# Turning the second batch's normalised rows through HBM and VectorE in an attention and mixture-of-experts kernel

## What is computed

```python
xn = layernorm(x)
qkv = xn @ w_qkv.T + b_qkv; q, k, v = split(qkv)
s = softmax(q @ k.T / sqrt(512)) @ v @ w_out.T + b_out
logits = xn @ router_w + router_b           # 8 experts, top 2, softmax of the two
combined = sum over the 2 experts of weight * silu(xn @ expert_w[e] + expert_b[e])
y = xn + combined @ proj_w + proj_b
g = silu(norm_w * y / sqrt(mean(y * y) + 1e-6))
out = x + s * g
```

## Time and profile before

| | before |
|---|---|
| median of 3 runs | 485.66 us (485.57 to 486.53) |
| profiled execution | 484.21 us |
| its span, first to last instruction | 482.5 us |
| TensorE (PE) busy | 474.7 us, 98% |
| VectorE (DVE) busy | 315.7 us, 65% |
| ScalarE (ACT) busy | 214.0 us, 44% |
| GpSimd (POOL) busy | 217.6 us, 45% |
| TensorE's mean granted clock | 0.997 of full |
| DMA | 115.79 MB, 240 GB/s mean |

### The profile page before, as it was taken

How to read it: one execution, slowest core, us unless ns; L and a number is a source line. 1 busy time by engine, 2 the same in 40 slices (tenths; PEclk the granted TensorE clock), 3 DMA queues, 4 the chain that set the end, 5 groups by cost and what they waited for, 6 DMA issues and landing times.

```text
span 482.5 us, 7168 instructions
## 1 busy us (share of the span) xinstructions
PE 474.7 (98%) x2168; PEld 391.9 (81%) x2169; DVE 315.7 (65%) x471; ACT 214.0 (44%) x310; POOL 217.6 (45%) x318
## 2 busy tenths in 40 slices
PE   9999999999999999999999999999999999999995
PEld 7878777888888888888888888888888888888884
DVE  4965352776734446898888889753588665857653
ACT  3673563143230264644644444333655452554540
POOL 5685010007887859500400000664478873476234
PEclk9999999999999999999999999999999999999998
DMA  8956999956979599978789666996555874455412
GB/s 312 353 210 253 382 348 410 357 186 235 324 243 334 186 320 308 285 212 259 230 269 263 201 191 176 338 315 246 151 176 174 239 198 151 123 190 172 149 46 86
DMA packets 78192, 115.79 MB, mean 240 GB/s; under 512 B 6657, under 2 KB 36369, under 8 KB 78161
## 3 DMA queue, kind: packets, MB, share of 16 engines
q1 hardware_dynamic: 65072, 79.72, 52.5%
q0 software_dynamic: 6896, 23.36, 13.9%
q10 hardware_dynamic: 6192, 12.32, 7.3%
HBM read 66.09 MB, written 49.28 MB: 239 GB/s over the span
## 4 chain that ended last, share of the span: by engine, by line
PE 97%; DVE 1%; issue 1%; ACT 0%; DVEq 0%
PE ab L1662 22%; PE ab L1664 22%; PE ab L1663 22%; PE sc L1662 8%; PE sc L1664 7%; PE sc L1663 7%; PE tp L1668 2%; PE tp L1704 1%; PE tp L1763 1%; PE sc L1733 1%; PE sc L1774 1%; PE sc L1736 1%; PE ab L1686 0%; PE ab L1688 0%; DVE xt_l L1229 0%
## 5 line engine op out<-in xcount | busy, mean ns | idle before, releaser
L822 POOL DMA_INDIRECT y<-y_scratch,pos x32 | 33.3, 1042 | 77.7 <-DMA y_scratch<-yt_so 63.3
L1664 PE MATMUL ab<-W,st_l 128*128 x156 | 60.7, 389 | 0.0
L1663 PE MATMUL ab<-W,st_h 128*128 x156 | 60.7, 389 | 0.0
L1662 PE MATMUL ab<-W,st_h 128*128 x156 | 60.7, 389 | 0.0
L805 POOL DMA_INDIRECT rows_scratch<-xb,pos x32 | 31.2, 975 | 51.2 <-DVEq L1343 43.0
L1662 PE MATMUL sc<-xt_h,t_h 128*128 128x512 f32 x128 | 50.1, 391 | 0.0
L1664 PE MATMUL sc<-xt_h,t_l 128*128 128x512 f32 x128 | 49.9, 390 | 0.0
L1663 PE MATMUL sc<-xt_l,t_h 128*128 128x512 f32 x128 | 49.8, 389 | 0.0
L1081 ACT CAST st_h<-tp 128x512 fp32r<-128x512 f32 x39 | 22.9, 587 | 43.3 <-PE ab L1664 41.2
L1423 DVE TENSOR_REDUCE small<-sc 128x1 f32<-128x1024 f32 x16 | 19.5, 1221 | 24.7 <-PE sc L1664 24.4
L1664 PEld LDWEIGHTS ab<-W,st_l 128*128 128x128 f32 x156 | 29.3, 188 | 6.1
(11 more groups left out here) (286 smaller groups left out, 1227.4 us busy)
## 6 DMA issues: line engine op xcount, KB each, us to landing
rows_scratch<-xn ACTq DMA_DIRECT2D x3, 3328.0 KB, 20.1
xb<-in_expert_w POOLq DMA_DIRECT2D x6, 1024.0 KB, 10.1
xn<-rows_scratch SPq DMA_DIRECT2D x48, 128.0 KB, 3.1
xg<-rows_scratch SPq DMA_DIRECT2D x44, 128.0 KB, 3.1
y_scratch<-yt_own SPq DMA_DIRECT2D x20, 256.0 KB, 3.1
y_scratch<-yt_so SPq DMA_DIRECT2D x19, 256.0 KB, 3.1
p_scratch<-prob SPq DMA_DIRECT2D x9, 512.0 KB, 2.8
rows_scratch<-xs SPq DMA_DIRECT2D x16, 256.0 KB, 6.7
```

What stands on the lines that cost most here:

```text
L822: pool.indirect_dma_start(y[:, q, :], None, y_d, bass.IndirectOffsetOnAxis(pos[:, GB * s + p:GB * s + p + 1], 0))\
L1662: nc.tensor.matmul(dst, lh, rh, start=start, stop=False)
L1663: nc.tensor.matmul(dst, lh, rl, start=False, stop=False)
L1664: return nc.tensor.matmul(dst, ll, rh, start=False, stop=stop)
```

## The change

For batch 1 alone (tiles 8 to 15):

- ScalarE normalises each tile in place in `xb1`, so that its `normalise` waits for no slot of the ring `xs`. `row_stats` of batch 1 run one iteration earlier in the batch 0 loop.
- TensorE no longer transposes them. SyncE stores each tile as before, waits until a pair has landed, loads the pair back spread with four DMAs into `xb` (batch 0's x, dead by then), and VectorE transposes it into `tp` (`turn_spread`).
- The second half of batch 1 is split into `wk_h` and `wk_l` (free after the folds) and not into `bt_h` and `bt_l` again.
- TensorE's order of logits becomes (0,0), (0,1), (1,0), two `key_weights`, (1,1).
- ScalarE issues the first store of zeros alone; SyncE issues the other two, after the last spread load.
- The scatters begin with batch 1, straight from `xb1`; only batch 0's rows are reloaded.
- GpSimd's first two expert weight loads (into `xb`) wait for all turned tiles and not for the last normalised one.

```diff
@@ sync @@
+            def spread_pair(n):
+                g = GB + 2 * n
+                for k in (g, g + 1):
+                    sp.wait_ge(xn_st[k % 4], 16 * (k // 4 + 1))
+                for a in range(4):
+                    sp.dma_start(xb[32 * a:32 * (a + 1), 2 * n:2 * n + 2, :].rearrange("p t (r f) -> p (t r) f", r=4),
+                                 rows_q[home(g):home(g) + 2, a, :, :, :].rearrange("t s r f -> s (t r) f"))\
+                        .then_inc(x_in[n], 16)
...
-            for g in range(G):
+            for g in range(GB):
...
+            for g in range(GB, GB + 4):
+                store_row(g)
+            for n in range(KC):
+                spread_pair(n)
+                if n < 2:
+                    store_row(GB + 4 + 2 * n)
+                    store_row(GB + 5 + 2 * n)
+            for n in (1, 2):
+                clear_slots(sp, n)
...
-            for g in range(GB):
-                load_to_send(g)
@@ gpsimd @@
-            pool.wait_ge(xn_ready, G)
+            pool.wait_ge(t_done, G)
...
-            for g in range(G):
-                pool.wait_ge(send_in[g % GB], 16 * (g // GB + 1))
+            for n in range(G):
+                g = (n + GB) % G
+                if n >= GB:
+                    pool.wait_ge(send_in[g], 16)
@@ scalar @@
-                if g >= 4:
+                if 4 <= g < GB:
...
+                if g >= GB + QB:
+                    act.wait_ge(fold, 2 * KC)
...
-                if t >= GB - 3:
+                if t == GB - 3:
                     act.wait_ge(zero_set, 1)
-                    clear_slots(t - GB + 3)
+                    clear_slots(act, 0)
             act.wait_ge(ln_done, 3)
-            for g in range(GB, GB + 4):
+            for g in range(GB, GB + 6):
                 normalise(g)
             fold_high(KC)
             act.wait_ge(vecs, 2)
             nc.scalar.copy(bias_rows, ...)
+            normalise(GB + 6)
+            act.wait_ge(qk_split, 4)
             hi(GB)
+            normalise(GB + 7)
             hi(GB + 1)
             fold_high(KC + 1)
-            normalise(GB + 4)
-            normalise(GB + 5)
             hi(GB + 2)
             hi(GB + 3)
             fold_high(KC + 2)
-            normalise(GB + 6)
-            normalise(GB + 7)
             fold_high(KC + 3)
-            act.wait_ge(rt_done, 1)
             for g in range(GB + QB, G):
                 hi(g)
@@ vector @@
+            def turn_spread(g):
+                k = g - GB
+                dve.wait_ge(x_in[k // 2], 64 + 16 * (2 if k < 4 else 1))
+                dve.wait_ge(lo_done, g - 1)
+                vec.transpose(tp[:, g % 2, :, :].rearrange("p c (r s) -> p c r s", r=4),
+                              xb[:, k, :].rearrange("p (r q c) -> p c r q", r=4, c=KC)).then_inc(t_done, 1)
...
+            turn_spread(GB)
+            turn_spread(GB + 1)
             fold_low(KC)
             lo(GB)
+            turn_spread(GB + 2)
             lo(GB + 1)
+            turn_spread(GB + 3)
+            fold_biases()
             fold_low(KC + 1)
-            fold_biases()
             lo(GB + 2)
+            turn_spread(GB + 4)
             lo(GB + 3)
+            turn_spread(GB + 5)
             fold_low(KC + 2)
             fold_low(KC + 3)
-            for g in range(GB + QB, G):
-                lo(g)
+            lo(GB + 4)
+            turn_spread(GB + 6)
+            lo(GB + 5)
+            turn_spread(GB + 7)
+            lo(GB + 6)
+            lo(GB + 7)
@@ tensor @@
             bias_products()
-            turn(GB)
-            turn(GB + 1)
             fold_keys(FOLDS[1])
             turn_biases()
-            turn(GB + 2)
-            turn(GB + 3)
             fold_keys(FOLDS[2])
             fold_keys(FOLDS[3])
             pe.wait_ge(pre_done, 4)
-            pe.wait_ge(lo_done, GB + QB)
-            pe.wait_ge(fold_l, KC + 1 + FOLDS.index(2))
-            logit_rows(1, 0).then_inc(rt_done, 1)
-            turn(GB + QB)
-            turn(GB + QB + 1)
             pe.wait_ge(fold_l, KC + 1 + FOLDS.index(0))
             logit_rows(0, 0)
-            turn(GB + QB + 2)
-            turn(GB + QB + 3)
             pe.wait_ge(fold_l, KC + 1 + FOLDS.index(1))
             logit_rows(0, 1).then_inc(rt_done, 1)
+            pe.wait_ge(lo_done, GB + QB)
+            logit_rows(1, 0)
             pe.wait_ge(fold_l, 2 * KC)
             key_weights(0, 0, 0)
+            key_weights(0, 0, 1)
             pe.wait_ge(lo_done, G)
             logit_rows(1, 1).then_inc(rt_done, 1)
-            key_weights(0, 0, 1)
             key_weights(0, 0, 2)
```

More of the change, by code:

```diff
@@ L394, in by_fours, with turned_rows, clear_slots @@
             return v.rearrange("p (c q) -> p q c", c=KC)
+        def turned_rows(g):
+            w = slice(g % QB * P, (g % QB + 1) * P)
+            if g < GB:
+                return xt_h[:, :, g * P:(g + 1) * P], xt_l[:, :, g * P:(g + 1) * P]
+            if g < GB + QB:
+                return bt_h[:, :, w], bt_l[:, :, w]
+            return wk_h[:, :, w], wk_l[:, :, w]
+        def clear_slots(eng, n):
+            w = slice(n * SLOT_TILES // 3, (n + 1) * SLOT_TILES // 3)
+            eng.dma_start(rows_t[:, w, :], zeros.to_broadcast([P, w.stop - w.start, D])).then_inc(zero_in, 16)
         def weights(e):
@@ L532, in store_row @@
                 sp.wait_ge(xn_ready, g + 1)
-                sp.dma_start(rows_g[home(g)], xs[:, g % 4, :]).then_inc(xn_st[g % 4], 16)
+                sp.dma_start(rows_g[home(g)], xs[:, g % 4, :] if g < GB else xb1[:, g - GB, :])\
+                    .then_inc(xn_st[g % 4], 16)
+            def spread_pair(n):
[6 more added lines that the diff above has]
+                        .then_inc(x_in[n], 16)
             load_half(0)
-            for g in range(G):
+            for g in range(GB):
                 if g == 4:
@@ L544, in load_to_send @@
             def load_to_send(g):
-                if g >= GB:
-                    sp.wait_ge(sent[g % GB], 32)
-                sp.dma_start(sent_rows[:, g % GB, :], rows_g[home(g)]).then_inc(send_in[g % GB], 16)
+                sp.wait_ge(sent[g], 32)
+                sp.dma_start(sent_rows[:, g, :], rows_g[home(g)]).then_inc(send_in[g], 16)
             def load_pair(i, n, tiles=2):
@@ L590, in _ @@
             store_s(0)
-            for g in range(GB, GB + 4):
+            for g in range(4):
                 load_to_send(g)
             store_s(1)
-            load_to_send(GB + 4)
-            load_to_send(GB + 5)
+            load_to_send(4)
+            load_to_send(5)
             store_s(2)
-            load_to_send(GB + 6)
-            load_to_send(GB + 7)
+            load_to_send(6)
+            load_to_send(7)
             store_s(3)
@@ L806, in _ @@
                                             sent_rows[:, g % GB, :], None).then_inc(sent[g % GB], 16)
[L807 to L810, removed]
+                if n < 2 * KC:
+                    early_low(n // KC, n % KC)
+                elif n >= 3 * KC:
+                    early_low(2, n % KC)
             for c in range(KC):
@@ L911, in normalise @@
             def normalise(g):
[L912 removed]
+                if 4 <= g < GB:
                     act.wait_ge(t_done, g - 3)
                     act.wait_ge(xn_st[g % 4], 16 * (g // 4))
[L915 removed]
+                whole = xbs[g // GB][:, g % GB, :]
+                nc.scalar.activation(xs[:, g % 4, :] if g < GB else whole, whole, ACT.Identity, bias=shift[:, g:g + 1],
                                      scale=rstd[:, g:g + 1]).then_inc(xn_ready, 1)
@@ L935, in t_hi @@
                     .then_inc(ab_hi, 1)
-            def clear_slots(n):
-                w = slice(n * SLOT_TILES // 3, (n + 1) * SLOT_TILES // 3)
-                act.dma_start(rows_t[:, w, :], zeros.to_broadcast([P, w.stop - w.start, D])).then_inc(zero_in, 16)
             for c in range(1, KC):
@@ L1387, in _ @@
                     fold_value_bias()
-                if 2 <= t < 6:
-                    n = t - 2
+                if 1 <= t < 5:
+                    n = t - 1
                     for k in range(2 * n, 2 * n + 2):
@@ L1727, in logit_rows @@
             def logit_rows(b, m):
-                high, low = (xt_h, xt_l) if b == 0 else (bt_h, bt_l)
+                high, low = (xt_h, xt_l) if b == 0 else (bt_h, bt_l) if m == 0 else (wk_h, wk_l)
                 keys = slice(m * 512, (m + 1) * 512) if b == 0 else slice(0, 512)
```

10 lines of the change are left out of this document (4 added, 6 removed).

## The result

| | before | changed |
|---|---|---|
| median | 485.95 us (485.23 to 486.53, 6 runs) | 489.21 us (488.11 to 489.71, 6 runs) |
| profiled execution | 484.21 us, span 482.5 | 489.3 us, span 487.6 |
| TensorE's mean granted clock | 0.997 | 0.987 |

The changed kernel takes 1.0061 times as long (95% interval 1.0048 to 1.0075): slower by 3.3 us. The spans differ by 5.1 us, because the profiled execution of before lies 1.7 us under its median and that of the changed kernel on its own.

The account below looks back on a forecast made before the run. TensorE, busy 474.7 of 482.5 us, was taken as the bound. Saved work -4.2, new waits +5.2 and restarts +0.3 gave +1.3 us; on 485.66 that made 487.0 us, range 484.6 to 490.0.

Parts of the forecast that it names:

- TensorE never waits, so what is taken off it counts in full: TensorE, whole run: longest wait 1.1 us, at the start; removed transposes 3.9 us, in all 4.2 us saved.
- The first spread pair at x = 56.4: VectorE's first transpose of a reloaded batch 1 pair begins at 56.4 us, bounds 54.9 to 60.6; tile stores landed at 51.9.
- Rival 1: Zeros don't hold the tile stores: VectorE begins at 54.9, TensorE waits 3.7, sum -0.2 us, 485.5 us; chance 0.25.
- VectorE's chain of 13.1 us: VectorE's work from its first spread transpose to the end of fold 1's low part: 13.1 us.
- TensorE asks at 62.4 and 64.3: TensorE could begin logits (0,0) at 62.4 us and logits (0,1) at 64.3 us if operands were there.
- the formula: TensorE's waits before logits (0,0) and (0,1) together: x + 13.1 - 64.3, which is x - 51.2 = 5.2 us.
- Rival 4, the clock: Clock falls in TensorE's new waits: 1.9 us more for one set of logits, 3.7 for two; 488.9 to 490.7; chance 0.12.
- the two waits have work between them: Argument against a clock fall in TensorE's new waits of 2.5 and 2.7 us before the logits.
- Rival 3, the moved zeros: Moved zeros in SyncE's queue make the store of probabilities 0 land 2.7 late; 488.2 to 489.2 us; chance 0.10.
- my 97 for the end of the backlog: The 13.1 MB of zeros, `nw`, `mw` and expert weights, at 387 GB/s, gone 34 us later, at 97 us.
- the 1.5 us that I said would hide it: Slack for probabilities 0: `pt_l` of tile 0 done at 107.0, TensorE begins `attend_tile(0)` at 108.53.
- The carried-over 1.45 us: The runs' median stands 1.45 us above the profiled execution before the change; this difference was added to the forecast.

Follow-up runs that it names:

- kept-busy kernel: The changed kernel plus 22 unread matmuls on TensorE, 14 before logits (0,0) and 8 before logits (0,1); 490.32 us, 1.0081.
- reordered kernel: The changed kernel with the fold stretch's work in another order on VectorE, ScalarE and TensorE, in several forms; 489.96, 489.56, 482.81 and 482.90 us.
- kept busy with zeros early: The changed kernel with 22 unread TensorE matmuls and the first two stores of zeros on ScalarE in iterations 2 and 5; 488.02 us, 1.0035.
- rows stored before: The changed kernel with spread loads reading batch 0's rows, stored long before, so they needn't wait for batch 1's stores; 485.27 us, 0.9984.
- the first reordered one: The changed kernel, same DMAs and instructions, VectorE doing folds' low parts early with transposes between, logits turned last; 489.96 us, 1.0086.
- the kernel with all zeros late: The changed kernel with the first store of zeros on SyncE too, all three behind the spread loads; 495.15 us, 1.0193.

## Why the prediction was right, by its own steps

It forecast slower, 487.0 us in a range of 484.6 to 490.0; 489.21 came. The place was right, the size lies in the range's upper part, and that it lies inside at all is in part luck, as the last item says.

- **TensorE never waits, so what is taken off it counts in full.** Right: the 3.9 us stand in the balance as they were read from the earlier trace rows.
- **The first spread pair at x = 56.4.** It was 58.45. ScalarE's normalisations ended on time (the first two stores were issued from 47.89, forecast 48.3 for the second). The mis-sized term is the stores: landed by 54.15, forecast 51.9. They took 5.5 us, between the 2.0 and the 7.7 of the earlier trace rows. Rival 1, with its 54.9, is refuted: without any zeros x was 56.0, with its stretch 0.6 earlier, and a tile's store took 3.7 us for 5.5. So the zeros hold the stores by 1.8 us, but a store in a burst of tiles isn't 2.0 us even with the DMA quiet; it is 3.7. The 4.6 us from landing to transpose of the earlier trace rows were 4.3.
- **VectorE's chain of 13.1 us.** 12.8 from 58.45 to the end of fold 1's low part at 71.3. Right. That ScalarE's high parts stand behind the same transposes was not in the prediction; they cost nothing here.
- **TensorE asks at 62.4 and 64.3.** At 62.9 and 64.8, later by 0.5, of which 0.4 is the stretch's later beginning. In the formula, 64.8 for 64.3 and 71.36 for 69.5: 6.6 us in place of 5.2. Two waits were forecast, 2.5 and 2.7; there were 3.9 and 0.8. With the later x the first became longer, and the second shorter, since the slow clock stretched the work between them.
- **Rival 4, the clock.** I gave it 0.12, and it is what came. Its price for one set of logits, 1.9 us, is what was measured (1.9 in the balance, 2.0 by the kept-busy kernel). The step that failed is "the two waits have work between them": the first alone was long enough, since the clock fell within it, and in three experiments so was a single wait of 2.3 to 2.4 us. The tail of the earlier trace rows had shown a fall about 2 us after the work ceased; I had the row and gave it too little.
- **Rival 3, the moved zeros.** Not the cause of this result: in the changed kernel `attend_tile(0)` doesn't wait (it begins at 113.55 and `pt_l` is done at 112.50). But my 97 for the end of the backlog was wrong; by the landings of the store behind it, it ended near 104. Two things go that way: the two stores of zeros were issued at 65.4 and not at 63, and the DMA moved only 102 to 313 GB/s between 54 and 68. What was left of the 1.5 us that I said would hide it was 1.0. It is the bound that every improvement of the fold stretch meets next, with 6.3 us in the clearest case.
- **The carried-over 1.45 us** between profiled execution and median did not carry over: the changed kernel's profiled execution lies at its median. By spans the loss is 5.1, by medians 3.3; my sum, +1.3, is short by 3.8 or by 2.0. On the median of 485.66 from which I set out, 5.1 more would be 490.8, outside the range: the misses in x and in the clock were made up for by an execution of before that happened to be fast. The terms that I can name for the first are x and the chain (1.4), the clock (1.9), and the late start with other small things (0.5).

Still open: why the wait near 180 us is 1.2 in one kernel, 0.3 in another and absent in a third. No run varied it alone. ScalarE's and VectorE's orders were changed together in every reordered kernel, so the share of each is not known.

## What to carry to other kernels

An operation that waits for a round trip through HBM must not stand at the head of an in-order engine with wanted work behind it; the detour here cost its lateness in front of `fold_low`, not its instructions, and with another order and two stores of zeros early the kernel was 0.6% faster than before. Look at both engines that make an operand: the high part stood behind the same detour as the low part. When a stall is removed, look at once at the next queue: large stores without a deadline that are put ahead of a small one with a deadline set the time at which the small one lands, even if it is issued 7 us sooner. And price a new wait of TensorE not by its length alone, but also by the work behind it at half clock.

## What the runs showed of the hardware that I had not expected

- A single standstill of TensorE of 2.3 to 2.4 us was enough for the granted clock to fall in three kernels (kept busy with zeros early, rows stored before, the first reordered one). In the kernel with all zeros late a first one of 2.33 us brought no fall, and a second of 2.39 did. One of 1.5 us brought none (one kernel). The clock stayed at the lower level for 3 to 10 us of mostly busy TensorE.
- A 512 KB store behind two stores of zeros, of `nw` and of `mw` on the same queue took 11 us at the most. In four kernels whose zeros are issued from 64.8 to 65.8 on, its issue lay at 93.1, 96.3, 98.9 and 100.4, and its landing at 104.0, 102.9, 103.9 and 103.8.
- ScalarE was held 6.2 us at the issue of a third store of zeros while two were under way, SyncE for 4.9 to 8.6 us at the store of `nw` behind two of zeros, and 9.1 us behind three.
